# Expert numbers of TensorE: one load of all 23 ahead of the slots, and the slots written out

## What is computed

```python
logits = x @ router_w.T
top_vals, top_idx = jax.lax.top_k(logits, 1)
expert_weights = jax.nn.sigmoid(top_vals)
dense_w = jnp.zeros((T, E), x.dtype).at[jnp.arange(T)[:, None], top_idx].set(expert_weights)
for e in range(E):
    y = silu(x @ w1[e]) * (x @ v1[e]) @ w2[e]
    out = out + dense_w[:, e:e + 1] * y
out = out + _glu(x, shared_gate.T, shared_up.T, shared_down.T)
```

## Time and profile before

| | us |
|---|---|
| median of 3 runs | 733.7 |
| fastest run | 732.82 |
| the profiled execution, its own time | 735.13 |
| its span | 733.2 |

### The profile page before, as it was taken

How to read it: one execution, slowest core, us unless ns; L and a number is a source line. 1 busy time by engine, 2 the same in 40 slices (tenths; PEclk the granted TensorE clock), 3 DMA queues, 4 the chain that set the end, 5 groups by cost and what they waited for, 6 DMA issues and landing times.

```text
span 733.2 us, 16347 instructions
## 1 busy us (share of the span) xinstructions
PE 620.5 (85%) x4645; PEld 463.8 (63%) x4647; DVE 531.9 (73%) x1217; ACT 386.5 (53%) x796; POOL 323.0 (44%) x672
## 2 busy tenths in 40 slices
PE   6899999987889899988999777999999667827776
PEld 5787888864444475566777566888887433315554
DVE  4688888873999986325222678899998458779994
ACT  2567777662111123234232264777776438779993
POOL 1223222233999642711111554333333258667772
PEclk9899999999999999999999998999999669969999
DMA  8901400000343100274541213000000000000011
GB/s 302 415 35 31 167 0 0 0 1 6 53 57 57 29 1 0 102 235 132 152 135 50 59 36 109 2 1 0 1 0 1 2 0 1 0 0 1 14 46 57
DMA packets 27342, 42.00 MB, mean 57 GB/s; under 512 B 3520, under 2 KB 22608, under 8 KB 26400
## 3 DMA queue, kind: packets, MB, share of 16 engines
q1 hardware_dynamic: 23808, 31.14, 14.4%
q0 software_dynamic: 3488, 10.28, 4.1%
HBM read 31.15 MB, written 10.26 MB: 56 GB/s over the span
## 4 chain that ended last, share of the span: by engine, by line
PE 61%; issue 12%; ACT 9%; DVE 8%; POOL 5%; DMA 3%; SPq 1%; DVEq 0%; POOLq 0%; ACTq 0%
PE ps L321 9%; PE ps L1124 5%; PE ps L349 5%; PE ps L331 4%; PE ps L313 4%; PE ps L359 4%; PE ps L369 4%; PE ps L713 4%; PE ps L1132 2%; PE ps L386 2%; PE ps L339 2%; POOL sorted_x L1185 2%; ACT wide L473 2%; ACT work L1718 2%; ACT wide L1689 2%
## 5 line engine op out<-in xcount | busy, mean ns | idle before, releaser
L230 POOL TENSOR_TENSOR var_eps<-mv,powers 128x1 f32<-128x1 f32 x80 | 16.8, 209 | 215.2 <-DVE mv L221 215.0
L473 ACT COPY wide<-ps 128x512 f32<-128x512 f32 x128 | 75.1, 587 | 60.9 <-PE ps L321 60.9
L321 PE MATMUL ps<-ident,work 128*128 128x128 f32 x512 | 84.0, 288 | 10.0 <-ACT wide L473 9.0
L545 DVE TENSOR_REDUCE work<-ps 128x8 f32<-128x1024 f32 x64 | 77.9, 1218 | 12.4 <-PE ps L313 12.4
L321 PEld LDWEIGHTS ps<-ident,work 128*128 128x128 f32 x512 | 56.4, 144 | 36.5 <-issue 29.3
L551 DVE TENSOR_TENSOR work<-ps,work 128x1024 f32<-128x1024 f32 x64 | 77.9, 1217 | 0.8 <-issue 0.2
L713 PE MATMUL ps<-ctxT,small 128*128 128x512 f32 (+1 forms) x192 | 65.7, 493 | 8.0 <-DVE ctx_sb L819 3.1
L468 ACT ACTIVATE work<-work 128x1024 f32<-128x1024 f32 x64 | 67.9, 1061 | 8.1 <-DVE work L551 7.5
L713 PEld LDWEIGHTS ps<-ctxT,small 128*128 128x128 f32 x192 | 35.3, 190 | 37.7 <-issue 28.0
L1158 DVE TENSOR_TENSOR work<-work,ps 128x256 f32<-128x256 f32 x23 | 9.7, 421 | 56.6 <-ACT work L1152 56.6
L349 PE MATMUL ps<-xnT,w_qkv 128*128 128x128 f32 x256 | 38.3, 298 | 11.5 <-DVE work L551 9.8
(11 more groups left out here) (207 smaller groups left out, 1556.5 us busy)
## 6 DMA issues: line engine op xcount, KB each, us to landing
wide<-in_expert_gu SPq DMA_DIRECT2D x1, 4096.0 KB, 20.8
small<-hank SPq DMA_DIRECT2D x32, 128.0 KB, 3.8
sorted_x<-small POOLq DMA_DIRECT2D x1, 2944.0 KB, 12.5
work<-sorted_x SPq DMA_DIRECT2D x23, 128.0 KB, 2.1
sorted_y<-work POOLq DMA_DIRECT2D x23, 128.0 KB, 2.4
xn_all<-in_ctx_rev_t SPq DMA_DIRECT2D x1, 2048.0 KB, 10.7
wide<-in_expert_d SPq DMA_DIRECT2D x1, 2048.0 KB, 25.3
xn_all<-in_ffn_w SPq DMA_DIRECT2D x2, 1024.0 KB, 6.3
```

Source lines behind the costliest of these rows:

```text
L321: mm = pe.transpose(T[:, h * P:(h + 1) * P], prob[r][:, h * P:(h + 1) * P], ident)
L473: act.copy(probT[r], T).then_inc(s["pT"], 1)
L545: dve.tensor_reduce(mxs[:, 8 * g:8 * g + 8], S2[g], AX.X, ALU.max).then_inc(s["mx"], 1)
```

## The change

`pe_slot` takes its expert numbers from a list instead of loading them. The list is made by one call behind the wait for `expert`, which loads all 23 numbers into registers of TensorE's sequencer, with the same bounds (0 to 7) as each single load had. And TensorE's bodies are written out in a Python loop over all 24, with the work beside bodies 2 to 5 as before; the other engines keep their loops. No other engine's program changes.

```diff
--- before.py
+++ after.py
@@ -1101,12 +1101,11 @@
                     mm = pe.transpose(ps[4][:, c * P:(c + 1) * P], xs[u][:, c * P:(c + 1) * P], ident)
                 mm.then_inc(s["xsT_ps"], 1)
 
-            def pe_slot(pe, t, u, i):
-                load = lambda t: pe.value_load(expert_of[0:1, ds(t, 1)], min_val=0, max_val=NE - 1)
+            def pe_slot(pe, t, u, i, experts):
                 if in_range(t):
-                    expert = load(t)
+                    expert = experts[t]
                 if in_range(t - 1):
-                    expert_y = load(t - 1)
+                    expert_y = experts[t - 1]
                 if in_range(t + 1):
                     pe_turn_slot(pe, t + 1, 1 - u, i + u)
                 if in_range(t - 1):
@@ -1231,11 +1230,16 @@
                 pieces(pe, pe_piece)
                 pe_shared(pe, 0, DOWN_FIRST)
                 pe.wait_ge(s["expert"], 1)
+                experts = nc.values_load_multi_w_load_instructions(
+                    expert_of[0:1, :], engines=[mybir.EngineType.PE], min_val=0, max_val=NE - 1)[1]
                 pe.wait_ge(s["sh_h"], 10)
                 pe.wait_ge(s["x_shared"], 2 + DOWN_FIRST)
                 keep_busy(pe, ps[5], ident, 12)
                 pe_turn_slot(pe, 0, 0, 0)
-                slots("pe", pe, pe_slot, 1, 1)
+                for t in range(NS + 1):
+                    pe_slot(pe, t, t % 2, t // 2, experts)
+                    if 2 <= t < 6:
+                        beside_slots("pe", pe, t - 2)
                 pe.wait_ge(s["silu"], NS)
                 pe_shared(pe, DOWN_FIRST, NB)
```

## The result

The change made the kernel slower: a median of 746.8 us against 734.4 (of four runs, the one of 3345 us among them), ratio 1.0172 with the 95% interval 1.0142 to 1.0203. The forecast was 740.1 with a range of 732 to 746, so the direction was right and the size was not. The profiled execution of the change took 747.24 us, with a span of 745.6.

What follows compares the result with a forecast made beforehand. Register loads and the data ring were taken to set the slots' pace. Slot 0 late 8.6, clock 1.8, gain 4.0: +6.4 us, so 741.5 for the profiled execution, 740.1 on the median's scale; range 732 to 746.

Steps and rivals of the forecast that it cites:

- The gain in the slots: Expert slots without register loads: 2.9 us in bodies 7 to 21 plus 1.1 behind L1491, sum 4.0 us.
- The ring's two periods: Slots' data ring, gate and up through silu, h and its transposes to next gate and up: 3.30 and 3.13 us alternately.
- The straight code: TensorE's written-out slots: costed at nothing, hidden by the sequencer's lead; without that cover, 1.6 us.
- What is hidden of the block: Ahead of slot 0: 1.6 us under the wait, 0.4 under the transfer; slot 0 late by L - 1.9.
- L: Time of the new load and checks before keep_busy: 3.6 load, 6.9 checks, 10.5 us; bounds 4.2 to 15.0.
- the rival of the full price: Before keep_busy: block really 23 loads and checks, L 15.0, 744.6 us; smaller gain and slower clock 746.8; chance 0.15.
- The clock: At keep_busy: TensorE's idling drops its clock to about half for 3.4 us, adding 1.8 us; bounds 0 and 2.6.
- The rest of the program: Stretches ahead of the block and behind the slots: no term of their own; the slots' gain handed on in full.

Runs made afterwards that it cites:

- written out only: Kernel before with TensorE's slots written out, its 46 loads left where they were; ratio 0.9917 (0.9885 to 0.9949) against the kernel before.
- the run with single loads: The change with 23 loads of one number each, each with its check, instead of one load of 23; ratio 1.0169 against the kernel before.
- the third run: The change itself, unaltered, traced a third time, on chip c beside the kernel before; 743.3 us against 733.8, ratio 1.0151.
- chip b: One of three chips used; the change itself ran again there beside the kernel before, ratio 1.013 (1.0096 to 1.0164).
- without checks: The change with the 23 numbers' bounds declared but not checked on the chip; ratio 0.9981, and 1.003 when run again, against the kernel before.
- one load per slot: The change without its block: each number loaded once in its slot's body and kept for the next; ratio 0.9925, again 0.9924 (728.1 us against 735.6).

## Why the prediction was wrong, step by step

*The gain in the slots* was right: 2.9 us were forecast for bodies 7 to 21, and 2.97 came (47.94 to 44.97); behind L1491 1.1 and 1.2. The ring's two periods came out at 3.29 and 3.12. The slots give 4.2 us; forecast 4.0.

*The straight code* shows no cost, as forecast (written out only). That most of the loads' exposure came from the branch ahead of them, and not from both loads, I had not separated: written out alone gives 2.3 us of the slots.

*What is hidden of the block* was right: with the measured L, L - 1.9 and the 1.4 that keep_busy lost make 12.2, and 12.0 was measured.

*L* is the term of the sum that was mis-sized: 10.5 forecast, 12.7 measured. The checks were 6.6 for 6.9. The load was 6.03 for 3.6. I had split the single load's 0.30 us into half a trip made once and half a share of each register, with nothing in the trace that showed such a trip. The register is nearly all of it (0.25 to 0.26 of 0.30). The upper bound, 23 times the single load, was 0.9 us away, the lower 5.7. The nearer price of the load was at hand, in the rival of the full price. That rival was not right either: its L of 15.0 is as far above the measured 12.7 as the forecast's 10.5 is below it, because 15.0 is the price of 23 single loads, as the run with single loads measured, and in bulk each number costs 0.1 us less. That its upper figure, 746.8, is the measured median is luck: too long a block and too small a gain stand there for terms that it did not have.
The Trainium skill's page "Runtime: NRT & Kernel Launch", section "Instruction fetch mechanics", has about 200 ns per register even in bulk, for device memory. The estimate by it, 4.6 us, was nearer than my choice of 3.6. The trace does not agree with it for on-chip memory: it shows 262 ns per register.

*The clock* was counted in one place only. keep_busy lost 1.4 us, forecast 1.8. Not forecast: behind it, the longer wait for the x of slot 4 (1.3 us more up to gate and up of slot 3; why its transfer took longer is open) and the fall of the clock at 338.0 (1.6 us more over slot 3). That takes 2.8 us of the slots' 4.2 in this trace, and in the trace of the third run too (81.9 both times), but not on chip b (79.5), nor without checks (79.0).

*The rest of the program* was taken as unmoved. The traces on record have -2.9 us ahead and +4.6 us behind, together +1.7. The repeats show that these stretches vary by more than that from trace to trace, with the clock; that none of it is the change's they do not show.

The sum, from the forecast's +6.4: +2.2 for L, -0.4 for keep_busy, -0.2 for the gain, +2.8 in the first slots, +1.7 elsewhere: +12.5, measured 12.4. The range ended at 746 because it left out the top of the full price, and the clock's term in it, 2.6 us at most, had no place for a second fall behind keep_busy.

Left open: by ratio "written out only" and "one load per slot" won 5.6 to 6.2 us, and their slots 2.3 to 3.4. The intervals reach down to 3.3 and 3.8 us. Whether something beyond the slots comes with them, or only the clock, the runs do not tell.

## What to carry to other kernels

Here a register load and its bounds check cost TensorE's sequencer 0.65 us, whether loaded singly or, but for 0.1 us, in bulk. Below a queue of matmuls that is free; in front of an empty queue nearly all of it is paid, with the clock's fall on top. So spread such loads, one per step, where work is still queued and ahead of a wait in which the queue runs dry, and keep a number that the next step needs in its register. Before gathering anything "once, ahead", ask what covers it there, and for an instruction on n items that no row shows take n times the single one until a run says otherwise.

## What the runs showed of the hardware that was not expected

- A load of n registers from on-chip memory is hardly cheaper than n loads: 0.30 us for one, 0.77 to 1.19 for three or four, 5.6 to 6.0 for 23. A bounds check is two instructions and 0.29 us per number. The same single load took up to 0.78 us with the h transposes moved, and 0.30 again once it stood ahead of the wait.
- The same instructions took 298.7 to 304.7 us ahead of the slots, and 333.5 to 340.8 behind them, over sixteen traces, and the mean granted clock goes with it: 0.953 to 0.960 in the traces with 333.5 to 333.8 on the kernels without a block, 0.940 and 0.937 in those with 340.3 and 340.8. Where the clock falls differs from one trace to the next, and that is worth several us here, as much as an edit of this size; no run varied it by itself.
- On chips a and b the last of the sums at L1065 came 9.4 us later than on chip c and in the traces on record, in every kernel, while GpSimd's scatter was under way. This was not explained.
